# Both attentions of a two-layer transformer: shared query and key tiles, tables for the order of work, six probability buffers

## The reference

```python
scores = jnp.einsum('bhqd,bhkd->bhqk', q, k) * scale
scores = jnp.where(causal, -jnp.inf, scores)
attn = jax.nn.softmax(scores, axis=-1)
out = jnp.einsum('bhqk,bhkd->bhqd', attn, v)
```

## Time and profile before

| what | value |
|---|---|
| device time, median of 3 runs | 2079.33 us (2076.75 to 2080.83) |
| device time of the profiled execution | 2072.83 us |
| its span, first to last instruction | 2071.1 us |
| TensorE busy | 1879.1 us (91%) |
| VectorE busy | 1435.9 us (69%) |
| ScalarE busy | 1193.8 us (58%) |
| GpSimd busy | 622.0 us (30%) |
| mean granted TensorE clock | 0.950 |
| moved by DMA | 210.87 MB |

### The profile page before, as it was taken

The page is one execution under the profiler, slowest core; times in us unless marked ns, Lnnn a source line. Parts: engine busy times, 40 slices in busy tenths (PEclk is TensorE's granted clock), DMA queues, the critical chain, the costliest instruction groups (busy, mean ns, idle before and its releaser), DMA issues. The chain is left out here.

```text
span 2071.1 us, 39995 instructions
## 1 busy us (share of the span) xinstructions
PE 1879.1 (91%) x9924; PEld 1169.6 (56%) x9926; DVE 1435.9 (69%) x6257; ACT 1193.8 (58%) x2252; POOL 622.0 (30%) x955
## 2 busy tenths in 40 slices
PE   5799999999986729994899999999999999899998
PEld 3455555555536527872445555555555558678886
DVE  6788777777826827875766666666666636887776
ACT  5266666666664728981445555555555558555554
POOL 4011111111120774762011111111111110567665
PEclk9799999999995869996989999999999999999999
DMA  6423233433305112224946464655555512546562
GB/s 214 123 35 64 42 61 44 61 48 55 49 8 207 36 56 70 75 76 132 362 112 145 104 139 106 136 111 130 116 126 122 119 35 81 138 93 131 128 121 61
DMA packets 107198, 210.87 MB, mean 102 GB/s; under 512 B 16540, under 2 KB 46378, under 8 KB 105680
## 3 DMA queue, kind: packets, MB, share of 16 engines
q1 hardware_dynamic: 99840, 194.98, 40.8%
q0 software_dynamic: 4992, 8.48, 1.3%
q10 hardware_dynamic: 2256, 6.21, 1.0%
HBM read 163.01 MB, written 47.89 MB: 102 GB/s over the span
## 5 line engine op out<-in xcount | busy, mean ns | idle before, releaser
L679 DVE CUSTOM_DVE_ANT_0 a1ms<-a1S,mask_q 128x128 bf16<-128x128 f32 (+1 forms) x758 | 387.9, 553 | 173.5 <-issue 170.6
L736 ACT ACTIVATE a1work<-a1T 128x512 f32<-128x512 f32 x576 | 330.2, 597 | 297.4 <-PE a1T L838 296.9
L679 DVE CUSTOM_DVE_ANT_0 a0ms<-a0S,mask_q 128x384 bf16<-128x384 f32 (+2 forms) x752 | 379.7, 553 | 97.5 <-issue 90.4
L736 ACT ACTIVATE a0work<-a0T 128x512 f32<-128x512 f32 x576 | 330.0, 597 | 186.6 <-PE a0T L838 175.7
L817 PE MATMUL a1O<-a1work,a1v 128*33 128x512 f32 (+3 forms) x1536 | 304.6, 496 | 0.9 <-POOL a1work L647 0.9
L838 PE MATMUL a0T<-a0qT,a0kT 128*128 128x512 f32 (+3 forms) x768 | 265.3, 392 | 15.9 <-ACT a0work L736 5.1
L838 PE MATMUL a1T<-a1qT,a1kT 97*128 97x512 f32 (+3 forms) x768 | 263.3, 391 | 2.0 <-DMA a1qT<-a1mr 2.0
L838 PEld LDWEIGHTS a1T<-a1qT,a1kT 97*128 97x128 f32 x768 | 131.6, 189 | 202.0 <-ACT a1work L736 144.5
L777 PE MATMUL a0S<-a0kS,a0qS 128*128 128x384 f32 (+2 forms) x752 | 229.9, 362 | 17.2 <-PEq L305 9.1
L1997 POOL TENSOR_TENSOR attn<-attn 128x512 f32<-128x512 f32 x136 | 201.4, 1496 | 105.8 <-DVE attn L1899 104.7
L838 PEld LDWEIGHTS a0T<-a0qT,a0kT 128*128 128x128 f32 x768 | 131.4, 189 | 170.2 <-ACT a0work L736 126.5
(11 more groups left out here) (336 smaller groups left out, 3333.2 us busy)
## 6 DMA issues: line engine op xcount, KB each, us to landing
attn<-scr_g SPq DMA_DIRECT2D x32, 1024.0 KB, 9.8
a1qT<-scr_q SPq DMA_DIRECT2D x93, 256.0 KB, 4.1
a1qS<-scr_q SPq DMA_DIRECT2D x90, 256.0 KB, 6.3
a1kT<-scr_k SPq DMA_DIRECT2D x93, 128.0 KB, 4.8
a1kS<-scr_k SPq DMA_DIRECT2D x90, 128.0 KB, 7.0
scr_q<-p_own SPq DMA_DIRECT2D x16, 512.0 KB, 5.1
scr_q<-attn SPq DMA_DIRECT2D x16, 512.0 KB, 7.4
scr_slots<-wp SPq DMA_DIRECT2D x1, 5980.0 KB, 18.2
```

The source lines that it names most:

```text
L679: nc.vector.tensor_tensor_reduce(masked_s[spare][:, 0:c1 - c0], buf[:, 0:c1 - c0], k.mask_q[:, SEQ - w + c0:SEQ - w + c1], 1.0, NEVER, ALU ...
L736: nc.scalar.activation(prob_of(g, p)[:, h, :], t_ps[slot % 2][:, :], ACT.Exp, scale=scale)\
```

## The change

1. One set of query and key tiles, three deep (`q`, `k`), serves both maxima and exponentials. `load` brings a group once; group g+2 goes into the tile of group g-1, once step g has its first scores (`st_ready`). Values keep two tiles and a load of their own (`load_v`). Maxima use rows 0 to 95 in both attentions (`SROWS`).
2. Units and value groups stand in slots given by tables (`ORDER_0`, `ORDER_1`: order of a head's blocks, place of the turn of the maxima, slot of each unit, slot of each piece's values, slots of the two output halves). The two halves of a block row and the two output halves are placed one by one. LEAD counts six units (before: four blocks, of which two are wide, so six units as well).
3. Six probability buffers in place of three.
4. The second half's reduction starts from the first half's result (`floor`), so the merge L686 goes; the second half waits for the first.
5. A loop pass holds six steps. In the first attention six steps stand ahead of it, one pass and four steps follow; in the second six, four passes and two.
6. In `project_0`, VectorE sets row 96 of the third key tile to one as well; GpSimd zeroes three tiles in place of five; ScalarE issues the queries and keys of the first two groups once each.

```diff
@@ class Operands
-        self.load_q, self.load_k, self.load_v = load_q, load_k, load_v
-        tiles = lambda n, heads: [c.enter_context(nc.sbuf_tensor(f"{name}{n}{i}", [P, heads, SEQ], F32R)) for i in range(2)]
-        self.qS, self.kS, self.qT, self.kT = tiles("qS", HG), tiles("kS", self.KH), tiles("qT", HG), tiles("kT", self.KH)
-        self.vst = [c.enter_context(nc.sbuf_tensor(f"{name}v{i}", [P, TPB, self.KH, VD + 1], F32)) for i in range(2)]
-        self.ldS, self.ldT = ([k.sem(f"{name}ld{n}{i}") for i in range(2)] for n in "ST")
-    def load_S(self, sp, g):
-        self.load_q(sp, self.qS[g[1]], g, self.ldS[g[1]])
-        self.load_k(sp, self.kS[g[1]], g, self.ldS[g[1]])
-    def load_T(self, sp, g):
-        self.load_q(sp, self.qT[g[1]], g, self.ldT[g[1]])
-        self.load_k(sp, self.kT[g[1]], g, self.ldT[g[1]])
-        self.load_v(sp, self.vst[g[1]], g, self.ldT[g[1]])
+        self.read_q, self.read_k, self.read_v = load_q, load_k, load_v
+        tiles = lambda n, heads: [c.enter_context(nc.sbuf_tensor(f"{name}{n}{i}", [P, heads, SEQ], F32R)) for i in range(3)]
+        self.q, self.k = tiles("q", HG), tiles("k", self.KH)
+        self.v = [c.enter_context(nc.sbuf_tensor(f"{name}v{i}", [P, TPB, self.KH, VD + 1], F32)) for i in range(2)]
+        self.loaded, self.v_loaded = [k.sem(f"{name}ld{i}") for i in range(3)], k.sem(f"{name}ldv")
+    def load(self, sp, g):
+        i = g[1] % 3
+        self.read_q(sp, self.q[i], g, self.loaded[i])
+        self.read_k(sp, self.k[i], g, self.loaded[i])
+    def load_v(self, sp, g):
+        self.read_v(sp, self.v[g[1] % 2], g, self.v_loaded)
+    def here(self, g):
+        return self.loaded[g[1] % 3], 16 * self.NLOAD * (g[0] * (GROUPS // 3) + (g[1] // 3 + 1))
...
@@ project_0, VectorE
-                nc.vector.memset(operands.kS[1][:, :, :].bitcast(F32), 0.0).then_inc(combined, 1)
+                nc.vector.memset(operands.k[2][:, :, :].bitcast(F32), 0.0).then_inc(combined, 1)
+                dve.wait_ge(combined, 1)
+                nc.vector.memset(operands.k[2][operands.MROW:operands.MROW + 1, :, :].bitcast(F32), 1.0).then_inc(combined, 1)
@@ project_0, ScalarE
-                        operands.load_S(act, (0, 0))
+                        operands.load(act, (0, 0))
                     elif s == 4:
...
-                        operands.load_T(act, (0, 0))
+                        operands.load_v(act, (0, 0))
                     elif s == 5:
...
-                        operands.load_S(act, (0, 1))
+                        operands.load(act, (0, 1))
@@ tables
+ORDER_0 = Order(((1, 0), (7, 0), (6, 0), (4, 0), (5, 0), (6, 1), (5, 1), (0, 0), (7, 1), (3, 0), (2, 0), (4, 1)),
+                2,
+                (0, 0, 1, 1, 2, 2, 4, 4, 5, 5, 6, 6, 6, 7, 9, 10, 10, 10, 10, 12, 12, 13, 14, 15, 16, 17, 18, 18, 19, 19, 20,
+                 20, 23, 23, 23, 23, 24, 25, 25, 26, 28, 28, 29, 29, 30, 31, 31, 32, 32, 33, 33, 34),
+                (11, 17, 21, 27, 27, 30, 35, 39, 44), (13, 15))
...
+PBUF_0, PBUF_1 = 6, 6
@@ attention
-    SROWS, TROWS = (MROW, MROW + 1) if KH == 1 else (P, P)
+    SROWS, TROWS = MROW, MROW + 1 if KH == 1 else P
-    LEAD = 4
+    LEAD = 6
-    PBUF = 3 * BURST if BURST == 1 else 2 * BURST
...
+    ahead_units = [(*x, a, slot) for (x, a), slot in zip([(x, 1) for x in chain[LEAD:]] + [(x, 2) for x in chain[:LEAD]], order.units)]
+    out_units = [("o", 0, 0, half, -1, slot) for half, slot in enumerate(order.outs)]
+    last_outs = [("o", 0, 0, half, 0, 0) for half in range(HALVES)]
...
+    for p, s in enumerate(order.values):
+        (VALUES[s] if s < NSLOT else CARRIED[s - NSLOT]).append(p)
+    COPY_AT = [order.values[p] + 1 for p in LAST_OF_BANK]
@@ main_steps
-            step((0, 0))
-            step((0, 1))
-            with eng.Fori(1, NG // 2 - 1) as u:
-                step((u, 0))
-                step((u, 1))
-            step((NG // 2 - 1, 0))
-            step((NG // 2 - 1, 1))
-        END = (NG // 2 - 1, 1)
+            for r in range(GROUPS):
+                step((0, r))
+            with eng.Fori(1, 1 + IN_LOOP) as u:
+                for r in range(GROUPS):
+                    step((u, r))
+            for r in range(NG - GROUPS * (1 + IN_LOOP)):
+                step((1 + IN_LOOP, r))
+        IN_LOOP = (NG - GROUPS - 2) // GROUPS
@@ SyncE
+                    if not at(g, NG - 2) and not at(g, NG - 1):
+                        if not at(g, 0):
+                            sp.wait_ge(st_ready, nth(g, NSLOT, 0))
+                        operands.load(sp, later(g, 2))
                     if not at(g, 0) and not at(g, NG - 1):
-                        sp.wait_ge(pv_done, lin(g, NP, 0))
-                        operands.load_T(sp, after(g, 1))
-                    if not at(g, NG - 2) and not at(g, NG - 1):
-                        sp.wait_ge(red_done, lin(g, NRED, NRED))
-                        operands.load_S(sp, after(g, 2))
+                        sp.wait_ge(pv_done, nth(g, NP, 0))
+                        operands.load_v(sp, later(g, 1))
                     if not at(g, NG - 1):
                         for h in range(HG):
-                            set_row(sp, after(g, 1), h)
+                            set_row(sp, later(g, 1), h)
@@ VectorE
+                            if half:
+                                dve.wait_ge(red_done, nth(gU, NRED, MAXIMA[h, i, 0]))
                             dve.wait_ge(unit_ready, base + (n + 1))
                             nc.vector.memset(held[:, spare:spare + 1], 0.0).then_inc(red_done, 1)
                             found = mhalf[par][:, h, i - TPB // 2:i - TPB // 2 + 1] if wide and half == 0 else mmax[par][:, h, i:i + 1]
+                            floor = NEVER
+                            if half:
+                                floor = mhalf[par][:, h, i - TPB // 2:i - TPB // 2 + 1]
                             nc.vector.tensor_tensor_reduce(masked_s[spare][:, 0:c1 - c0], buf[:, 0:c1 - c0],
-                                                           k.mask_q[:, SEQ - w + c0:SEQ - w + c1], 1.0, NEVER,
+                                                           k.mask_q[:, SEQ - w + c0:SEQ - w + c1], 1.0, floor,
                                                            ALU.add, ALU.max, found).then_inc(red_done, 1)
-                            if i == BLOCKS[-1] and HALVES == 2:
-                                dve.wait_ge(red_done, lin(gU, NRED, MAXIMA[h, i, half] - 1))
-                                upper = mmax[par][:, h, TPB // 2:TPB]
-                                nc.vector.tensor_tensor(upper, upper, mhalf[par][:, h, :], ALU.max).then_inc(red_done, 1)
```

263 lines of the change are left out of this document (125 added, 138 removed).

## The result

The changed kernel takes **1995.41 us** (median of 4 runs, 1988.71 to 1998.16) against 2078.04 us for the kernel before on the same chip (2072.73 to 2080.83): a ratio of 0.960, 95% interval 0.957 to 0.963. The forecast was 1995. Single runs lie up to 7 us from the median, so an agreement to 0.4 us is luck in part. The profiled execution took 1993.72 us (span 1992.0), so profile against profile 79.1 us are gone, where my sum said 84.

A forecast was written before the change was run, and what follows sets the result against it. TensorE, busy for 91% of the span, was taken as the bound. Savings of 28 + 41 + 6.3 + 6.6 + 1.6 + 1 = 84 us against the median of 2079.33 gave 1995 us, range 1966 to 2032.

The forecast's parts named there:

- Joined groups, second attention: Second attention: four joins of value groups per step at 0.31 us each, net 0.9 us per step, 28 us over 31 steps.
- Loop: First attention: five loop returns of 1.26 us go, 6.3 us saved; second attention's returns already covered, nothing.
- Tables, first attention: First attention: units placed by tables cut waits by 2.4 us per step, 2.7 with one join, 41 us in all.
- the waits stay: Rival, first attention: with two psum tiles all 3.8 us of waits per step remain, 38 us less saved, 2033; chance 0.13.
- Start waits: Start of both attentions: TensorE's waits for the row of maxima, 4.58 and 2.03 us, both go, 6.6 us saved.
- Merges: Openings of both attentions: dropped merges of the halves' maxima save 1.3 us in the first and 0.3 in the second.
- Ahead of the first attention: Before the first attention: VectorE's extra memset plus 3.0 us, fewer loads minus 2 to 4; net minus 1.
- The projection ahead of the second attention: Projection stage before the second attention: no change in time claimed.
- The rival of the flanks: Rival, both attentions: a join saves only its flanks, first weight load stays exposed; 14 us less saved, 2009; chance 0.15.
- The other rivals: First-attention waits stay, 2033, chance 0.13; VectorE starves TensorE, 2138, 0.05; loads of queries and keys late, 2080, 0.02.
- a starvation of TensorE: Rival, both attentions: TensorE waits on VectorE for banks in bursts of units, 143 us, so 2138; chance 0.05.
- TensorE still never idle: Sign of a right prediction: in the second attention TensorE has no idle time, with steps of 19.6 us.

## Why the prediction was right, and where it was not

The time came out as forecast to 0.4 us of the median, and that is luck: two terms of 7 and 8 us that I had put at nothing, and smaller ones that came out too high, were made up for by joins and first-attention steps that gave more. The saving itself was 82.6 us by the medians and 79.1 us profile against profile, where the recorded terms add up to 84.5. By the steps of the sum:

- **Joined groups, second attention: 28 us.** Mechanism and price hold: 0.31 forecast, 0.30 measured by taking the joins away, 1.84 and 2.71 us for the clusters. The step was mis-sized: 1.24 us each instead of 0.9, since I had charged 0.25 for waits and 0.1 for an output's turn that the trace of after does not show. It would be 36 us over 29 steps.
- **Loop.** The step that failed: "In the second attention TensorE is never idle, so the returns are already covered there: nothing." They cost 8.2 us of those 36, though they had cost nothing before (both loops written out left it at 20.48). I took the cover from the old order and did not ask what a return costs in the new one. It is not the shorter step or the clusters that uncovered them, since without joins they cost 11.9 us. What a return costs is a wait of TensorE, 1.4 to 2.1 us with what follows, and often a fall of the granted clock behind it, with which the return costs 3.1 to 5.1 us. Why TensorE waits is open: ScalarE and VectorE both pause at the return (VectorE 3.77, 2.96 and 3.15 us, where the kernel before has pauses of 1.31 us at most, the same in steps with and without a return), a pass is six steps long instead of two, and four units now stand in slot 0. That the first wait is for the exponential and not for a bank speaks for the pauses; no run parts these. In the first attention, loop, loads and merges together gave 9.8 us where I had 6.3; how these share it is open, since with the old loads the loop's stall is partly replaced by late keys. The Trainium skill, "Runtime: NRT & Kernel Launch", section "Instruction fetch mechanics", says that a taken branch outside the fetched window forces a fetch before work goes on, while straight code is streamed at a cost that is mostly hidden. The run without the loop agrees: the three long steps are gone, 8.2 us, some of it the clock's.
- **Tables, first attention: 41 us.** 2.77 a step against 2.7, shown by putting the placement back. The walk with two psum tiles was good enough; "the waits stay" is excluded.
- **Start waits: 6.6 us.** Too high by 1.4 us or more: the first attention's row of maxima is still waited for in most profiles, not in that of after. So this profile's step 0, 32.6 us, is a lucky one: in the six where TensorE waited 1.5 to 1.8 us it is 34.2 to 35.4. The second attention's wait is gone, as I had said.
- **Merges: 1.6 us.** Wrong: nothing came. The opening is 28.1 us long, 28.0 before. The reductions that replace the merges take 0.06 us longer, 16 times in the opening, which takes back 0.9 of the 1.3 us of four merges; the rest is not accounted for.
- **Ahead of the first attention: 1 us, between +3 and -3.** Measured +0.3, a loss and not a gain, as the sum of -3.9 and +4.2; the second is larger than the 3.0 I had.
- **The projection ahead of the second attention: "I leave at nothing."** It failed: 6.9 us. The change removes a third of ScalarE's issues there and so moves the others in time, onto other stores of SyncE. Moving them off the stores gave 3.3 and 5.5 us of it back. They had overlapped stores before as well, at no such price; what makes the difference is open. I had not followed the queues in that stage.

Measured: first attention 55.3, second 30.0, behind it 1.1, less 6.9, less 0.4 at the start and the openings: 79.1. The rival of the flanks is refuted by 0.14 us saved inside a join of two. The other rivals did not occur in the changed kernel; a starvation of TensorE did as soon as the clusters were evened out, and cost 146 us. "TensorE still never idle", which was to show the prediction right, failed: 4.7 us in 440, at the returns above all.

## What to carry to other kernels

Joining column-tiled groups saves a turn of 0.3 us each on a full TensorE, up to the point where the engines fed by the scores run dry; that point is near: one join more cost 0.5 us a step net, two more 4.7 us, where four had given 1.2. A stall that was hidden under the old order, as the loop's returns were, has to be priced again under the new one, here at 8 us. A wait of about one microsecond on a full TensorE is worth looking at for what follows it: with the clock's fall the loss was twice or three times as large. When a change takes DMAs off a queue in an untouched stage, look at what the rest of that queue will now meet.

## What was not expected of the hardware

- A masked reduction that starts from a value per partition takes 58 ns more than one from a constant (744 against 686 ns at 512 columns).
- Six DMAs issued by ScalarE took 2.7 us alone and 7.0 us beside SyncE's issues, which took 1.0 us and more each. In the kernel before, six took 2.8 us although SyncE was issuing too; there two of SyncE's took 3.3 and 3.4 us.
- A return of the same loop over the same code cost 3.7, 1.5 and 3.1 us in one execution. The granted clock fell to 0.50 behind the first and the third, not behind the second.
- A memset of one row of 4096 elements takes 3.47 us, as long as one of 128 rows.
- After 1.35 us of waiting in an otherwise full stretch the granted clock fell to 0.57 on average of 4 us, and a cluster took 4.47 us instead of 2.77.
